# A fused graph and expert kernel: the statistics of the last four gated groups moved into gating steps 1 to 4, and the tanh of most units made a second time into PSUM

## What is computed

```python
def _gru_cell(inp, h, w_ih, w_hh, b_ih, b_hh):
    gi = inp @ w_ih.T + b_ih
    gh = h @ w_hh.T + b_hh
    i_r, i_z, i_n = jnp.split(gi, 3, axis=-1)
    h_r, h_z, h_n = jnp.split(gh, 3, axis=-1)
    r = jax.nn.sigmoid(i_r + h_r)
    z = jax.nn.sigmoid(i_z + h_z)
    n = jnp.tanh(i_n + r * h_n)
    return (1.0 - z) * n + z * h

h = layernorm(x)
for i in range(3):
    m = h @ weight[i]
    aggr = jnp.einsum('bst,bsd->btd', A, m)
    h = _gru_cell(aggr, h, w_ih, w_hh, b_ih, b_hh)
x = x + h
xf = layernorm(x)
H = gelu(xf @ W1 + b1)
probs = softmax(H @ Wg + bg)
out = x + probs[assign] * (H @ Wd[assign] + bd[assign])   # assign = argmax(probs)
```

## Time and profile before

| | before |
|---|---|
| median of 3 runs | 492.2 us (490.88 to 492.68) |
| the profiled execution | 492.83 us |
| its span, first to last instruction | 491.1 us |
| mean granted clock of TensorE | 0.992 |
| busy: PE, PEld | 465.0 us (95%), 383.5 us (78%) |
| busy: DVE, ACT, POOL | 367.6 us (75%), 309.9 us (63%), 383.6 us (78%) |

### The profile page before, as it was taken

How to read it: one execution, slowest core, us unless ns; L and a number is a source line. 1 busy time by engine, 2 the same in 40 slices (tenths; PEclk the granted TensorE clock), 3 DMA queues, 4 the chain that set the end, 5 groups by cost and what they waited for, 6 DMA issues and landing times.

```text
span 491.1 us, 10198 instructions
## 1 busy us (share of the span) xinstructions
PE 465.0 (95%) x3055; PEld 383.5 (78%) x3055; DVE 367.6 (75%) x1153; ACT 309.9 (63%) x547; POOL 383.6 (78%) x375
## 2 busy tenths in 40 slices
PE   8999999999899998999999969999999999999994
PEld 4778878887787786788788747777669999999994
DVE  4789778898697997798977968788787555655552
ACT  3865876667666568766777857888663554445531
POOL 4479997899979899889988675777777777377576
PEclk9999999999999999999999998999999999999998
DMA  7611445311136221111111200111352342233110
GB/s 211 179 45 46 138 135 165 99 54 53 36 104 208 65 62 42 48 43 44 54 55 49 60 29 26 43 62 56 111 146 86 116 131 91 65 102 90 33 50 22
DMA packets 65013, 39.96 MB, mean 81 GB/s; under 512 B 9260, under 2 KB 61616, under 8 KB 64960
## 3 DMA queue, kind: packets, MB, share of 16 engines
q1 hardware_dynamic: 59040, 29.99, 21.6%
q0 software_dynamic: 4320, 8.93, 5.2%
q10 hardware_dynamic: 1600, 0.40, 0.4%
HBM read 17.12 MB, written 10.04 MB: 55 GB/s over the span
## 4 chain that ended last, share of the span: by engine, by line
PE 54%; POOL 23%; DVE 8%; issue 5%; ACT 3%; SPq 3%; DMA 2%; POOLq 0%; DVEq 0%; ACTq 0%
PE bank L750 12%; PE bank L522 10%; PE bank L523 10%; PE bank L524 10%; POOL diff L405 5%; POOL diff L407 5%; POOL hT_lo L427 4%; PE bank L553 3%; POOL mv L457 2%; PE bank L687 2%; POOL xrow L412 2%; PE bank L736 2%; SPq L318 1%; DVE hn L1136 1%; POOL xrow L470 1%
## 5 line engine op out<-in xcount | busy, mean ns | idle before, releaser
L953 ACT ACTIVATE adj_i<-bank,b1c 128x512 f32<-128x512 f32 (+1 forms) x136 | 91.1, 685 | 74.1 <-PE bank L524 73.5
L405 POOL TENSOR_TENSOR diff<-hT,n_sb 128x512 f32<-128x512 f32 x48 | 75.0, 1562 | 18.1 <-ACT n_sb L848 18.1
L489 POOL DMA_INDIRECT sorted_rows<-xrow,pos x64 | 62.0, 968 | 25.5 <-issue 23.7
L750 PE MATMUL bank<-wd_sb,adj_i 128*128 x568 | 66.7, 275 | 0.0
L407 POOL TENSOR_TENSOR diff<-z_sb,diff 128x512 f32<-128x512 f32 x48 | 63.4, 1320 | 3.8
L750 PEld LDWEIGHTS bank<-wd_sb,adj_i 128*128 128x128 f32 x568 | 65.1, 192 | 0.3 <-issue 0.3
L522 PE MATMUL bank<-hT_hi,whh_hi 128*128 128x512 f32 x132 | 55.9, 424 | 5.1 <-issue 5.1
L522 PE MATMUL bank<-ag_hi,wf_hi 128*128 128x512 f32 x144 | 58.8, 408 | 1.8 <-DVE ag_lo L1115 1.7
L522 PE MATMUL bank<-hT_hi,w_hi 128*128 128x512 f32 (+1 forms) x136 | 58.8, 432 | 0.9 <-ACT adj_i L953 0.7
L523 PE MATMUL bank<-ag_lo,wf_hi 128*128 128x512 f32 x144 | 57.0, 396 | 0.0
L524 PE MATMUL bank<-ag_hi,wf_lo 128*128 128x512 f32 x144 | 56.9, 395 | 0.0
(11 more groups left out here) (175 smaller groups left out, 1050.0 us busy)
## 6 DMA issues: line engine op xcount, KB each, us to landing
bands<-hT SPq DMA_DIRECT2D x192, 64.0 KB, 2.2
adj_i<-sorted_rows SPq DMA_DIRECT2D x71, 72.0 KB
xrow<-in_x_dram SPq DMA_DIRECT2D x16, 256.0 KB, 3.2
adj_i<-in_adj_dram SPq DMA_DIRECT2D x16, 256.0 KB, 3.6
sorted_rows<-xrow,pos POOLq DMA_INDIRECT x64, 2.3
sorted_rows<-padrow SPq DMA_DIRECT2D x9, 72.0 KB
out_dram<-cand,home POOLq DMA_INDIRECT x39, 2.3
bd_bc<-in_L_ffn_bd_dram SPq DMA_DIRECT2D x1, 512.0 KB, 3.3
```

Of the source, the lines that this page charges most:

```text
L405: nc.gpsimd.tensor_tensor(diff[:, b, :], hT[:, g, :], n_sb[:, b, :], ALU.subtract).then_inc(diff_ok, 1)
L489: nc.gpsimd.indirect_dma_start(out=sorted_rows, out_offset=bass.IndirectOffsetOnAxis(ap=pos[:, g, j:j + 1], axis=0), in_=xrow[:, g * GR + ...
L750: last = nc.tensor.matmul(o, HT[:, sg % 2, k, j * P:(j + 1) * P], wd_sb[:, bass.ds(at + k * P, P)], start=(k == 0), stop=(k == KC - 1))
L953: nc.scalar.activation(HT[:, hb, k, 0:n], HB[k][:, 0:n], ACT.Gelu, bias=b1c[:, k:k + 1]).then_inc(done, 1)
```

## The change

**Tanh in PSUM.** `new_state_psum(u)` makes tanh(cand + bias) once more and writes it to bank pF (even units) or pX (odd). ScalarE issues it for unit s-1 in step s, behind the two sigmoids. It waits for h_ok of unit u-2, the last reader of the bank. VectorE's `state(u)` then adds diff to the bank instead of n_sb, and waits for the new semaphore np_ok too. n_sb is still made, since GpSimd reads it. `in_psum` is true for units 4 and 5, 10 to 17, 22 to 29 and 34 to 45, which is 30 of 48; the units left out are those behind which ScalarE has `normalise` in step u+1, the first four and the last two. TensorE waits in gate step 1 for h_ok of unit 45, before logits are written to pX.

**Statistics.** `gate_measured` is gone. Groups 12, 13, 14 and 15 are measured in gate steps 1, 2, 3 and 4, between the routing instructions as group 15 was before. Each waits for x1_ok of its own group just before its first BN_STATS. GpSimd makes the row scales of groups 12 to 15 in gate step 5.

```diff
--- before.py
+++ after.py
@@ -175,6 +175,7 @@
             sem(n) for n in ("aghi_ok", "r_ok", "z_ok", "n_ok", "hthi_ok", "h0_ok", "h0hi_ok"))
         aglo_ok, h_ok, h0lo_ok, rhn_ok, cand_ok, x1_ok, adj_ok = (
             sem(n) for n in ("aglo_ok", "h_ok", "h0lo_ok", "rhn_ok", "cand_ok", "x1_ok", "adj_ok"))
+        np_ok = sem("np_ok")
         band_in, hn_ok = [sem("band_in"), sem("band_in_odd")], sem("hn_ok")
         bn_ok, mv_ok, var_ok, rstd_ok, xn_ok, shift_ok = (
             sem(n) for n in ("bn_ok", "mv_ok", "var_ok", "rstd_ok", "xn_ok", "shift_ok"))
@@ -263,6 +264,16 @@
         FIRST_LOADS = GROUPS // 2
         FFN_WEIGHTS = UN - 9
         GATE_ROWS = UN - 7
+
+        NB = (pF, pX)
+
+        def in_psum(u):
+
+            return QUAD <= u < UN - 2 and not first(u + 1 + ahead(u + 1)[NORMAL])
+
+        def summed(u):
+
+            return sum(in_psum(v) for v in range(u + 1))
 
         def landed(n, ways):
 
@@ -476,7 +487,7 @@
 
             def gate_step(s):
                 g = s - 3
-                if s == 4:
+                if s == 5:
                     row_scales(QUADS - 1)
                 if inside(g, GROUPS):
 
@@ -679,6 +690,7 @@
 
                     if s == 1:
                         pe.wait_ge(ffn_in, FFN_LOADS)
+                        pe.wait_ge(h_ok, UN - 2)
                     pe.wait_ge(g_h, s * KC)
                     hold(pe, g_lgT, s - 2)
                     for k in range(KC):
@@ -846,6 +858,10 @@
             def new_state(u):
                 hold(act, cand_ok, made("all", u))
                 nc.scalar.activation(n_sb[:, u % 2, :], cand[:, u % 2, :], ACT.Tanh, bias=bi[:, 2:3]).then_inc(n_ok, 1)
+
+            def new_state_psum(u):
+                hold(act, h_ok, made("all", u - 2))
+                nc.scalar.activation(NB[u % 2][:], cand[:, u % 2, :], ACT.Tanh, bias=bi[:, 2:3]).then_inc(np_ok, 1)
 
             def normalise(u):
                 act.wait_ge(shift_ok, 2 * (made("first", u) - ACT_UNITS))
@@ -934,6 +950,8 @@
                 if exists(s):
                     reset(s)
                     update(s)
+                if in_psum(s - 1):
+                    new_state_psum(s - 1)
                 if first(u):
                     rows_turned(u)
                 u = s - 2
@@ -1028,13 +1046,6 @@
 
             def gate_stats(g, j):
                 return nc.vector.bn_stats(gstats[:, g % 2, j, :], xres[:, g * GR + j, :])
-
-            def gate_measured(g):
-                dve.wait_ge(x1_ok, g + 1)
-                for j in range(GR):
-                    last = gate_stats(g, j)
-                last.then_inc(g_bn, 1)
-                gate_moments(g)
 
             def gate_moments(g):
                 dve.wait_ge(g_bn, g + 1)
@@ -1125,7 +1136,10 @@
 
             def state(u):
                 hold(dve, zd_ok, made("all", u))
-                tt(hT[:, u % QUAD, :], n_sb[:, u % 2, :], diff[:, u % 2, :], ALU.add).then_inc(h_ok, 1)
+                if in_psum(u):
+                    dve.wait_ge(np_ok, summed(u))
+                new = NB[u % 2][:] if in_psum(u) else n_sb[:, u % 2, :]
+                tt(hT[:, u % QUAD, :], new, diff[:, u % 2, :], ALU.add).then_inc(h_ok, 1)
 
             def state_rows(u):
                 b = u % 2
@@ -1207,16 +1221,11 @@
 
                 route, place = inside(s - 2, GROUPS), inside(s - 3, GROUPS)
                 turn, norm = inside(s + 1, GROUPS), inside(s + 3, GROUPS)
-                measured = GROUPS - 1
-                stat = s == 3
-                if stat:
-                    dve.wait_ge(x1_ok, GROUPS)
+                measured = GROUPS - QUAD - 1 + s
+                stat = inside(s - 1, QUAD)
                 b, d = (s - 2) % 2, (s - 3) % 2
                 n, m, k = (s - 2) * ROUTE, (s - 3) * PLACE, (s - 2) * SOFT
                 lg = lg4[:, b, :, :]
-                if s == 0:
-                    gate_measured(GROUPS - 4)
-
                 if route:
 
                     dve.wait_ge(g_lg, s - 1)
@@ -1241,6 +1250,7 @@
                     red(mx[:, b, :], lg, AX.X, ALU.max).then_inc(g_dve, 1)
                 if stat:
 
+                    dve.wait_ge(x1_ok, measured + 1)
                     gate_stats(measured, 0)
                 if route:
                     dve.wait_ge(g_dve, n + 1)
@@ -1303,8 +1313,6 @@
                 if route:
                     dve.wait_ge(g_pdve, k + 4)
                     nc.vector.reciprocal(xrow[:, (s - 2) * GR:(s - 1) * GR, PROB], ssum[:, b, :]).then_inc(g_prob, 1)
-                if s < 2:
-                    gate_measured(GROUPS - 3 + s)
                 if place:
                     dve.wait_ge(g_base, s - 2)
```

## The result

| | before | changed |
|---|---|---|
| median, from to | 491.99 us (490.88 to 492.68) | 486.91 us (485.75 to 488.06) |
| ratio, 95% interval | | 0.9899 (0.9880 to 0.9919) |
| the profiled execution | 492.83 us | 488.06 us |
| its span | 491.1 us | 486.3 us |
| granted clock of TensorE | 0.992 | 0.995 |

The account below looks back on a forecast made before the run. TensorE was busy 465.0 of 491.1 us; its holes came from POOL falling behind in the graph stage and from the passage to gating. 492.8 - 3.7 (graph stage) - 1.4 (passage) = 487.7 us, range 484.3 to 491.3.

Parts of the forecast that it names:

- The update from PSUM: VectorE's state update reading the tanh from PSUM: as long as the undisturbed one, 0.69 us, ends 0.65 and 0.75.
- The added tanh: ScalarE's second tanh, into PSUM, for 30 units: 0.65 us each, ends 0.6 and 0.75, in all 20 us.
- What POOL saves: Second and third first layers: five POOL instructions shorter by 2.03 us, chain begins 0.65 us later, net 1.4 us each.
- ScalarE late at steps 14, 26, 38: Steps where rows are turned and a state is split: ScalarE's longer queue costs 0.1 us three times, 0.3 us.
- Room on ScalarE: Plain graph-stage unit: 0.39 + 0.59 = 0.98 us of room for 0.6 us of new work, TensorE sees nothing.
- the slower rival: Graph stage: the added tanh exceeds ScalarE's room, at 1.2 us each PSUM unit loses 0.22; 495.4 us, chance 0.05.
- Graph stage 3.7 us: Gain of the tanh in PSUM: 4.0 us less 0.3 for ScalarE's longer queue; ends 1.5 and 4.8.
- Passage 1.4 us: Passage to gating: moved statistics let TensorE resume at 293.4 instead of 294.86 us; ends 0.3 and 2.9.
- The clock: Passage to gating: if the clock does not fall, the 1.7 us gained widens TensorE's hole at 354 and is lost.
- The hole at 354: TensorE's wait for rows loadable after POOL scattered eight groups: ends 1.4 us earlier, by what VectorE's step 3 gains.
- The rival of no effect in the graph stage: POOL holds the update despite its PSUM operand; the graph stage gives nothing and costs 0.3; 491.7 us, chance 0.10.
- The one of little: ScalarE's lateness is paid again at later units, graph stage gives 1.0, passage 0.3; 491.5 us, chance 0.15.

Follow-up runs that it names:

- Run 5: Changed kernel with ScalarE's added tanh into PSUM put behind the splitting of the state instead of ahead of it: 485.96 us, ratio 0.9872 to the kernel before.
- run 7: Changed kernel with one more tanh, into SBUF and read by nothing, ahead of the one into PSUM: 490.80 us, ratio 0.9968 to the kernel before.
- runs 2: Changed kernel with no unit's tanh in PSUM, only the moved statistics: 559.41 us on a slower chip, ratio 0.9983 to the kernel before.
- run 3: Changed kernel with the PSUM tanhs still made but VectorE's update reading n_sb: 560.44 us on a slower chip, ratio 0.9995 to the kernel before.
- run 10: Changed kernel with only the moved statistics, no tanh in PSUM, measured a second time: 558.05 us on a slower chip, ratio 0.9956 to the kernel before.
- run 6: Changed kernel with all units from 4 to 45 updated from PSUM, including those left out: 483.91 us, ratio 0.9820 to the kernel before.

## Why the prediction was right

487.7 us was forecast for the profiled execution and 488.06 came, 486.91 in the median; the range and the case are the ones named. Step by step:

- **The update from PSUM, 0.69 us.** 680 ns. The range of 0.65 to 0.75 held. The Trainium skill (VectorE: DVE Perf Modes, on SBUF-source operations) gives a PSUM source 62 cycles more. No row here shows it: the undisturbed updates with two SBUF operands, 29 of 48 before, were 0.66 to 0.69 us long, the one with a PSUM operand 680 ns in the mean.
- **The added tanh, 0.65 us, 20 us in all.** 682 ns and 20.5 us. It went into PSUM 38 ns faster than into SBUF (720 ns), which the prediction had only bounded. The Trainium skill (ScalarE: Activation LUTs, Step-by-step: what each stage is for) has this as a rule: PSUM is the quicker destination for ScalarE. The rows here agree.
- **What POOL saves, net 1.4 us at the second and third head.** 1.44 and 1.44. The working behind it holds too: 2.03 us of shorter instructions (in the chain of units 24 to 31 the L412 went from 2052 to 1596 ns, the L405 of unit 27 from 1756 to 1307, the L452 of unit 29 from 735 to 236), less one tanh ahead of the chain. Run 5 took away that one and got 0.60 and 0.64 back.
- **First head 0.5:** 0.44. **The fourth layer 0.7:** 0.58. There the small hole is closed.
- **ScalarE late at steps 14, 26, 38, 0.3 us in all.** At unit 15 the changed kernel is 0.16 us behind before, at unit 17 0.52 us ahead again. Over units 10 to 20 0.20 us are lost. The size is right, the places cannot be told apart.
- **Room on ScalarE, 0.98 us.** 1.04 us by run 7. So the slower rival was priced at about the right point, and 0.68 us is safely under it.
- **Graph stage 3.7 us.** 3.88. But the step with the experts' weights differs by up to 1.5 us between kernels in which nothing near it changed, so the figure is not as exact as it looks: without that step it is 3.4. That the two figures lie within 0.2 us is in part luck.
- **Passage 1.4 us.** 1.43 from unit 47's ag_lo to the first scatter, and runs 2, 3 and 10 give 1.5 for it. The hole at 287 gave nothing, as said. One thing was taken too low: of the two small instructions that were to be held by residuals, one was free (0.45 us), the other took 1.20, so TensorE's second hole gave 1.7 and not 1.4.
- **The clock.** It did not fall this time, and the 1.7 us that this might give were forecast not to arrive. They did not. The reason given was only half right. The hole at 354 was to grow by what TensorE won; it did not (1.18 us instead of 1.11), because the load of the sorted rows took 1.6 us less, which the prediction did not have. TensorE was 6.34 us ahead from there on, and yet the program ended 4.8 us sooner, as much as the first scatter came sooner (4.9). The likely reason is POOL's chain of 188 us, from the first scatter to the end of the program. "POOL scatters back to back from the first pos on" was read rightly, but only as far as the first eight groups. So the passage's 1.4 us came out as forecast, but by the reckoning of TensorE's hole, which as far as the runs show did not set the end; that is luck too.

The rival of no effect in the graph stage fell with run 3 beside the changed kernel. The one of little did not come either: the second and third heads gave 1.44 us each, so the chains do not pay for ScalarE's lateness a second time.

What the prediction did not see is what the change left lying. It took the choice of units as given, and its own rows had an L452 of unit 30 that "stays as it was". Of those twelve updates before the heads six (units 7, 8, 19, 20, 31 and 32) took 1.18 to 1.77 us in the changed kernel, and run 6 shows 3.9 us for the twelve.

## What to carry to other kernels

VectorE with two SBUF operands and GpSimd beside it slowed each other here. Moving one of VectorE's operands to PSUM freed both, and the gain is to be counted on the engine that is behind, instruction by instruction, with the price of whatever is now ahead of its first one. If some instructions are exempted to spare an engine, measure that engine's room: here twice the added work cost 0.35 us a step, and the exemption cost 1.3 us a head. Where one engine works off the last stage without a gap, count the gain at that engine's first instruction; what another engine won beyond that did not show in the time here.

## What the runs showed of the hardware

- The same tanh of 128x512 takes 682 ns into PSUM and 720 ns into SBUF (30 and 48 instructions; 684 and 682 ns in runs 3 and 7).
- One PSUM operand in VectorE's update is enough: 680 ns for 30 of them, 683 ns for the 42 of run 6, with POOL's long instructions beside them, while the ones with two SBUF operands took up to 2.05 us.
- On POOL an indirect DMA of 128 rows takes 1.27 to 1.29 us from one issue to the next, 0.30 us of it between two, with nothing to wait for.
- On two chips the program took 14% longer, and the profiles show it behind the first scatter. In run 10, from 300 to 488 us, TensorE is busy for 152.47 us at a granted clock of 0.86; in the profile of the kernel before that is shown above, for 182.13 at 1.00. The stretch of run 10:

```profile
300.00:488.00 188.00, 152.47 (x1145) 118.47 (x1145) 92.58 (x455) 77.84 (x145) 96.56 (x100) 0.86 0.21 62
```

Why is not known. The question who sets the end had no answer on those chips.
